# One block up to the output projection, score maxima of two groups inside the last projection steps, and pieces three slots later

## The reference, cut to what matters

```python
x = x + xattn(layernorm(x), ctx)        # x, ctx: [4, 1024, 512], fp32, 16 heads of 32
x = x + ffn(layernorm(x))
# xattn: q = x@Wq+bq, k = ctx@Wk+bk, v = ctx@Wv+bv
#   scores = q k^T / sqrt(32), -inf where masked, softmax over keys, @ v, @ Wo + bo
#   mask: three image chunks of 256 tokens attend within themselves; the last 256 (text)
#   tokens attend to all 768 image tokens and causally to text
# ffn: xq = fakequant(x)  with scale = sigmoid(clip) * max|x| / 127 over the WHOLE tensor
#   h = fakequant(silu(xq@Wg') * (xq@Wu'))  with a scale over the whole of h
#   out = h @ Wd'; Wg', Wu', Wd' are quantised row by row (1408 hidden units)
```

## Time and profile before

| | us |
|---|---|
| median of three runs (lowest, highest) | 1152.42 (1151.9, 1155.57) |
| the profiled execution | 1155.27 |
| its span, first to last instruction | 1153.5 |
| PE busy | 1062.2 (92%) |
| DVE / POOL / ACT busy | 750.1 / 640.9 / 512.5 |

### The profile page before, as it was taken

One profiled execution on the slowest core, in us unless ns is written; L12 is line 12 of the kernel. 1 busy time (PEld: TensorE's weight loads), 2 busy tenths in 40 slices (PEclk: granted clock), 3 DMA queues, 4 the chain that ended last, 5 costly groups with the idle time before them and its releaser, 6 DMA issues. The chain is left out here.

```text
span 1153.5 us, 18187 instructions
## 1 busy us (share of the span) xinstructions
PE 1062.2 (92%) x6527; PEld 704.8 (61%) x6550; DVE 750.1 (65%) x1340; ACT 512.5 (44%) x881; POOL 640.9 (56%) x345
## 2 busy tenths in 40 slices
PE   5999999999629989999999999899995799998898
PEld 4888888888516656666666666456763444443343
DVE  5665456654319757777777777236968477877785
ACT  3322223222101656666777666651110555553553
POOL 3434455344440979999999999555753113100373
PEclk9999999999955989999999999899997799999899
DMA  5987777856699896768888673449996353100876
GB/s 203 318 258 234 221 276 256 270 170 197 207 178 188 187 225 150 180 158 180 182 180 194 151 178 101 124 126 236 312 287 172 96 224 122 36 1 3 322 240 219
DMA packets 129619, 218.08 MB, mean 189 GB/s; under 512 B 29320, under 2 KB 55688, under 8 KB 128330
## 3 DMA queue, kind: packets, MB, share of 16 engines
q1 hardware_dynamic: 129546, 217.12, 68.1%
HBM read 134.76 MB, written 77.74 MB: 184 GB/s over the span
## 5 line engine op out<-in xcount | busy, mean ns | idle before, releaser
L775 ACT ACTIVATE a_probs<-a_banks 128x512 f32<-128x512 f32 (+2 forms) x512 | 233.9, 535 | 131.6 <-PE a_banks L991 106.6
L712 POOL TENSOR_TENSOR a_pair_sums<-a_probs,a_probs 128x2048 f32<-128x2048 f32 x48 | 223.6, 4658 | 66.3 <-ACT a_probs L775 57.6
L850 DVE TENSOR_REDUCE a_max<-a_banks 128x2 f32<-128x512 f32 x192 | 123.3, 685 | 53.8 <-PE a_banks L962 53.5
L991 PE MATMUL a_banks<-a_queries,a_keys 97*128 97x512 f32 x384 | 148.1, 429 | 10.4 <-ACT a_probs L775 5.7
L962 PE MATMUL a_banks<-a_keys,a_queries 96*128 96x256 f32 x384 | 86.0, 319 | 32.7 <-DMA a_queries<-q_split 32.7
L967 PE MATMUL a_banks<-a_keys,a_queries 96*128 96x512 f32 (+1 forms) x256 | 114.7, 462 | 0.0
L846 DVE CUSTOM_DVE_ANT_0 a_masked_scores<-a_banks,kept_mask 128x384 f32<-128x384 f32 (+1 forms) x128 | 79.5, 621 | 50.0 <-PE a_banks L967 49.7
L850 DVE TENSOR_REDUCE a_max_parts<-a_banks 128x1 f32<-128x512 f32 x128 | 87.9, 687 | 24.8 <-PE a_banks L967 20.9
L962 PEld LDWEIGHTS a_banks<-a_keys,a_queries 96*128 96x128 f32 x384 | 70.3, 205 | 54.5 <-DMA a_queries<-q_split 33.4
L1347 POOL TENSOR_TENSOR d_out<-d_out,f_x 128x512 f32<-128x512 f32 x28 | 42.6, 1548 | 99.1 <-DVE d_out L1375 99.1
L225 POOL TENSOR_SCALAR p_x<-p_x,p_neg_mean,p_rstd 128x512 f32<-128x512 f32 x32 | 28.2, 895 | 121.9 <-DVE p_rstd L330 121.9
(11 more groups left out here) (166 smaller groups left out, 2205.2 us busy)
## 6 DMA issues: line engine op xcount, KB each, us to landing
a_keys<-k_split SPq DMA_DIRECT2D x48, 512.0 KB, 8.5
a_queries<-q_split SPq DMA_DIRECT2D x48, 512.0 KB, 14.3
f_x<-x_scratch SPq DMA_DIRECT2D x14, 1024.0 KB, 7.8
p_c<-in_ctx_dram SPq DMA_DIRECT2D x8, 1024.0 KB, 8.8
p_x<-in_x_dram SPq DMA_DIRECT2D x8, 1024.0 KB, 10.9
v_scratch<-p_v_stage SPq DMA_DIRECT2D x16, 512.0 KB, 9.0
k_split<-p_stage_hi SPq DMA_DIRECT2D x16, 512.0 KB, 4.3
k_split<-p_stage_lo SPq DMA_DIRECT2D x16, 512.0 KB, 5.4
```

The costliest lines, as they stand in the source:

```text
L712: pool.tensor_tensor(PP[u % 2], PR[2 * c % 4], PR[(2 * c + 1) % 4], ALU.add).then_inc(paired, 1)
L775: act.activation(PR[kt % 4][:, j, 0:w], STB[:, n % NST, 0:w], ACT.Exp, scale=SCALE).then_inc(edone, 1)
L850: dve.tensor_reduce(out, src, AX.X, ALU.max).then_inc(wfree, 1)
L991: op = pe.matmul(out.rearrange("p (c t) -> p c t", t=SIT), keys, q, start=True, stop=True)
```

## The change

It does five things. (1) `project` and `attend_output` become one block, each engine running the first's instructions and then the second's without a meeting between. For that their memory is laid out anew: the projection has five banks instead of eight (the other three are the work banks of the pieces), one context buffer instead of two, one transposed pair each instead of two, two stage pairs for k and q together instead of four. (2) The 56 pieces of groups 0 and 1 and the turning of group 0's maxima go between the v and q items of steps 5, 6 and 7; their stacks are loaded part by part in steps 4 to 6. The keys of stack 1 lie where the x buffer and the context buffer are, and are loaded last in step 6. (3) The layernorm is cut in two (`moments`, `deviations`), which go behind the first and second k item. (4) Pieces start three slots later: those of group g run from slot 3 of group g-2 to slot 2 of group g-1; the turning is at slot 3; `shift_rows(i+1)` comes behind the store of slot 3. (5) In the feed-forward, the first chunk is quantised and turned in halves, one of the two copies behind it goes to DVE, the last group of h maxima is cut in two, and the first quantisation of `down` starts with one tile.

```diff
+NB = 5
+EARLY = 4
-TURN_SLOT = 1
+TURN_SLOT = 3
-GROUPS = ((0, 4), (4, 8), (8, IT))
+GROUPS = ((0, 4), (4, 8), (8, IT - 1), (IT - 1, IT))
+DOWN = [((0, 1), (1, 4), (4, 8), (8, IT))] + [((0, 4), (4, 8), (8, IT))] * (NCH - 1)
...
 # project, sync: step(b, u), late = n - 4 in steps 4 to 7
+                if late == 0:
+                    for q in sout:
+                        sp.wait_ge(q, 32 * 5)
                 for i in range(2):
                     s.reach(sp, free, NB + at(n) + VALUE + 2 * i + 2)
...
+                    if last and i == 0:
+                        A.shift_rows(sp, 0)
+                    A.load_early(sp, late, i)
...
+                stage_store(n, 0)
+                stage_store(n, 1)
+                A.load_early(sp, late, 2)
+                if last:
+                    for q in vout:
+                        sp.wait_ge(q, 16 * (NCH + 1))
+                    for i in range(2):
+                        A.load_values(sp, i)
+                    for part in range(3):
+                        A.load_stack(sp, 2, part)
+                if more(n, 2):
+                    s.reach(sp, free, NB + at(n) + CTURN + KT)
+                    load_c(n + 2)
+                stage_store(n, 2)
+                A.load_early(sp, late, 3)
+                stage_store(n, 3)
+                if late == 2:
+                    sp.wait_ge(full, at(n) + CTURN + KT)
+                    for part in range(3):
+                        A.load_stack(sp, 1, part)
+                if last:
+                    for part in range(3, 6):
+                        A.load_stack(sp, 2, part)
 # project, vector: step
                     dve.tensor_tensor(VST[t // 2][:, t % 2, :], bank(u, VALUE + t), BV, ALU.add).then_inc(free, 1)
+                    for i, k in A.early(n, t):
+                        A.largest(dve, i, k)
+                    if t == 0 and not more(n, 1):
+                        A.rows_out(dve, 0)
...
-                    layernorm(1 - u, n + 2, b if u == 0 else b + 1)
                 for j in range(KT):
-                    staged(u, n, KEY + j, j, 0, 1, KT + j)
+                    staged(u, n, KEY + j, j, 1, KT + j)
+                    if more(n, 1) and j == 0:
+                        moments(1 - u, n + 2, b + u)
+                    if more(n, 1) and j == 1:
+                        deviations(1 - u, n + 2)
                     ffn_rows(n, j)
 # project, tensor: step
                 for t in range(TT):
                     tokens_out("v", CT, t, claim(u, n, VALUE + t))
+                    for i, k in A.early(n, t):
+                        A.scores(pe, i, k)
+                    if t == 0 and not more(n, 1):
+                        A.turn_maxima(pe, 0)
...
 # attend_output
+        FIRST = [(n, item) for n, items in ((EARLY + 1, range(KT, 2 * KT)), (EARLY + 2, range(2 * KT)), (EARLY + 3, range(2 * KT)))
+                 for item in items]
+        COUNT = (3, 2, 2) * 4 + (4,) * 4 + (3,) * 4
-        def slot_pieces(kt):
-            first = sum(S_PER_SLOT[:kt])
-            return list(range(first, first + S_PER_SLOT[kt]))
+        def slot_pieces(i, kt):
+            slot = NKT * i + kt - TURN_SLOT
+            g, part = 2 + slot // NKT, slot % NKT
+            if slot < 0 or g >= NGRP:
+                return []
+            count = [S_PER_SLOT[(m + TURN_SLOT) % NKT] for m in range(NKT)]
+            first = sum(count[:part])
+            return [(g, k) for k in range(first, first + count[part])]
+        def load_early(sp, late, place):
+            part = 4 * late + place if late is not None else 9
+            if part < 6:
+                load_stack(sp, 0, part)
+            elif part < 9:
+                load_stack(sp, 1, part - 3)
 # attend_output, sync
-            for i in range(2):
-                load_stacks(i)
-                load_values(i)
-            shift_rows(0)
-            load_stacks(2)
-            load_values(2)
             for i in range(NGRP):
-                if i + 1 < NGRP:
-                    shift_rows(i + 1)
                 if i == 0:
-                    load_stacks(3)
-                    load_values(3)
+                    front.ffn_last(sp)
                 store(i, 0)
...
                 store(i, 1)
+                if i + 1 < NGRP:
+                    shift_rows(sp, i + 1)
+                if i == 0:
+                    for row in range(6):
+                        load_stack(sp, 3, row)
+                    sp.wait_ge(front.fst, 32 * (NCH + 1))
+                    for m in range(2, 4):
+                        load_values(sp, m)
...
                 sp.wait_ge(stfull, HG * NKT * (i + 1))
                 if i + 4 < NGRP:
-                    load_stacks(i + 4)
+                    for row in range(6):
+                        load_stack(sp, i + 4, row)
 # gate_up, tensor: the first chunk in halves
+            def turn_first():
+                for h in range(2):
+                    pe.wait_ge(xq, h + 1)
+                    for i in range(2):
+                        for k in range(2):
+                            for t in range(2 * h, 2 * h + 2):
+                                op = pe.transpose(TB[:, i, k, t * P:(t + 1) * P],
+                                                  XQ[0][:, t, (2 * i + k) * P:(2 * i + k + 1) * P], K.ident_b[:])
+                        if h:
+                            op.then_inc(turned, 1)
```

More of the change, by code:

```diff
@@ new lines, with __init__, place, stack @@
+S_ITEMS = 7
+S_PER_SLOT = (3, 3, 4, 4, 4, 3, 4, 3)
+TURN_SLOT = 3
+AHEAD = 3
+QROWS = 3 * DH
+NGRP = BATCH * G
+NST, NWK = 3, 3
+STACK, TILE = HG * N, KT * C
+GROUPS = ((0, 4), (4, 8), (8, IT - 1), (IT - 1, IT))
+DOWN = [((0, 1), (1, 4), (4, 8), (8, IT))] + [((0, 4), (4, 8), (8, IT))] * (NCH - 1)
+RES = 6
+class Kept:
+    pass
+class Memory:
+    def __init__(self, s):
+        self.nc, self.at = s.nc, {}
+        for name, words in (("arena_a", RES * IT * CH), ("arena_b", 9 * TILE)):
+            s.sb(name, [P, words])
+            self.at[name] = s.nc.sbuf_base - 4 * words
+    def place(self, name, arena, word, shape, dt=F32):
+        return self.nc.alloc_sbuf_tensor_at(name, shape, dt, offset=self.at[arena] + 4 * word)[:]
+    def stack(self, name, i, half, word, shape, dt=F32):
+        return self.place(name, "arena_a", (2 * i + half) * STACK + word, shape, dt)
+    def rest(self, name, word, shape, dt=F32):
+        return self.place(name, "arena_a", 8 * STACK + word, shape, dt)
+    def over(self, name, word, shape, dt=F32):
+        return self.place(name, "arena_b", word, shape, dt)
@@ L181, in step @@
                     load_x(n + 2, u)
-                for i in range(4):
-                    item = KEY + 2 * i if i < 2 else query(final) + 2 * (i - 2)
-                    s.reach(sp, free, NB + at(n) + item + 2)
-                    dst = (ks, ks, qs, qs)[i]
-                    for part in range(2):
-                        d = dst[part].rearrange("(m p) t -> p m t", p=P)[:, 2 * (i % 2):2 * (i % 2) + 2, bass.ds(n * CH, CH)]
-                        sp.dma_start(d, f32(STG[i][part][:])).then_inc(sout[i], 16)
@@ new lines, in attend_output, with early @@
+        FIRST = [(n, item) for n, items in ((EARLY + 1, range(KT, 2 * KT)), (EARLY + 2, range(2 * KT)), (EARLY + 3, range(2 * KT)))
+                 for item in items]
+        COUNT = (3, 2, 2) * 4 + (4,) * 4 + (3,) * 4
+        def early(n, item):
+            if not isinstance(n, int) or (n, item) not in FIRST:
+                return ()
+            at = FIRST.index((n, item))
+            first = sum(COUNT[:at])
+            return [divmod(k, NPC) for k in range(first, first + COUNT[at])]
@@ L698, in _, with gpsimd @@
             sp.wait_ge(ldk, 32)
[L700 to L703 removed]
+        A.sync = sync
+        def gpsimd(pool, front):
             def pair(i, c):
@@ new lines, in attend_output, with scores @@
+        A.vector = vector
+        def scores(pe, i, k):
+            n = A.pieces
+            j, m = PIECES[k]
+            if k == 0:
+                pe.wait_ge(stk[i % 4], LOADS * (i // 4 + 1))
+            pe.wait_ge(wfree, n + 1)
+            out = WB[:, n % NWK, :]
+            keys = KS[i % 4][0:QROWS, j, :]
+            queries = lambda t: QS[i % 4][0:QROWS, j, t * P:(t + 1) * P]
+            if m < 3:
+                for half in range(2):
+                    op = pe.matmul(out[:, half * SIT:(half + 1) * SIT], queries(2 * m + half),
+                                   keys[:, m * SIT:(m + 1) * SIT], start=True, stop=True)
+            else:
+                t, part = 6 + (m - 3) // 2, (m - 3) % 2
+                k0, k1 = 512 * part, min(512 * (part + 1), (t + 1) * P)
+                op = pe.matmul(out[:, 0:k1 - k0], queries(t), keys[:, k0:k1], start=True, stop=True)
+            op.then_inc(wfull, 1)
+            A.pieces += 1
@@ L1004, in values @@
                     pe.wait_ge(ifree, 3 * i + kt // 2)
+                if kt == 0 and i == 0:
+                    for bank in (6, 7):
```

(3 more changed lines are left out.)

618 lines of the change are left out of this document (315 added, 303 removed).

## The result

The changed kernel takes 1199.88 us (median of 4 runs, 1196.25 to 1203.79) against 1153.54 for the kernel before: a ratio of 1.039, 95% interval 1.037 to 1.042. The forecast was 1156.5, with a range of 8 in 10 that ended at 1167. The number is wrong by 43 us; the sign is right, at a chance of 48% that the forecast gave it. The profiled run has 1196.25, its span 1194.5.

What follows compares the result with a forecast made beforehand. PE, busy 92% of the span, was taken to bound the kernel. The terms -22.9 + 8.8 + 19.8 + 2 - 3.6 = +4.1 moved the median from 1152.4 to 1156.5 us; range of 8 in 10: 1138 to 1167.

Steps and rivals of the forecast that it cites:

- Five banks: Projection steps 0 to 6: with five banks PE starts q 1.8 us late in each step, 12.6 us in all.
- Pieces between items: Between projection items: pieces with changes to and fro cost 14 us, waits for DVE and the turning 3.4 us.
- Keys of stack 1: Projection step 7: PE waits 10 us for these keys, plus 1.5 us of low clock, together 11.5 us.
- Last piece to group 1's second pass: Between these two points: burst of scores, slots and one wait take 20 us, against 24.7 before.
- the third rival: Queue shared with the projection gets worse: stores land late, ACT waits for stage buffers, +10 us, 1166.5; chance 13%.
- The backlog: Shift rows of group 2 come some 11 us late behind queued loads; groups 1 to 3 lose 8.8 us.
- What every group pays: Groups 3 to 14: waits of 0.9 us at the turning and 0.9 for shift rows, 19.8 us lost.
- Feed-forward: Quantisation in halves wins 1.7 us before the first matmul, a one-tile start in down 1.9; together -3.6 us.
- the first fell: Rival: waits in the groups, at slots 3 and 5, don't show; at most 0.3 us a group, 1140; chance 15%.
- the second fell: Rival: five banks are enough in the projection, DVE's order costs nothing, 1144 us; chance 14%.

Runs made afterwards that it cites:

- the best version: The kernel of e10, the fastest of all the runs: 1120.44 us, ratio 0.969 to the kernel before.
- e9: Changed kernel with shift rows before the store, pieces two slots later, stack 1 keys earlier, stacks one group later, layernorm before k items: 1126.97 us, ratio 0.975.
- e10: e9 with the key parts of stack 2 issued right behind the last step's v stores, ahead of the k stores: 1120.44 us, ratio 0.969.
- e5: Changed kernel with the key parts of stack 2 issued behind the last two q stores instead of ahead: 1196.41 us, ratio 1.037.
- e4: Changed kernel with stacks loaded one group later, behind the shift rows instead of ahead of them: 1180.93 us, ratio 1.023.
- e1: Changed kernel with the shift rows issued ahead of the output store that they followed: 1168.41 us, ratio 1.012.
- e2: Changed kernel with pieces two slots later instead of three, the turning staying at slot 3: 1182.23 us, ratio 1.027.
- e6: Changed kernel with moments, deviations and ACT's root ahead of the k items again, still with five banks: 1186.31 us, ratio 1.027.
- e7: Kernel before with only the pieces three slots later, the turning at slot 3 and shift rows behind slot 3's store: 1195.52 us, ratio 1.034.
- e13: e10 with shift rows behind slot 3's store again and one 512 KB stack part between them in groups 1 to 12: 1202.15 us, ratio 1.042.
- e3: Changed kernel with the keys of stack 1 issued ahead of both q stores of step 6: 1183.05 us, ratio 1.026.

## Why the prediction was wrong

**Five banks** (12.6 us). The wait was there in steps 0 to 6, for the reason given: 1.3 + 0.4 a step. Measured 2.1 a step (38.26 against 36.17), 14.7 for seven, and 3.3 more in the two steps whose clock fell: 5.4 too little. The layernorm ahead again takes 1.5 to 1.7 of the 2.1 away.

**Pieces between items** (17.4). Nearly right. In the best version the stretch from the x transposes of step 5 to the first score takes 121.9 us; before, to 307.2, it took 95.9. Of the 26.0 between them 3.2 are bank waits in step 5, some 1.2 are longer steps, and 3.3 are the clock, which was low in step 5 behind those waits (clock 0.93 in the row above; the transposes behind the waits took 1.2 us more than elsewhere, the q items behind them 1.9 and 0.2). That leaves 18.3: 3.7 of waits for DVE (3.4 forecast) and 14.6 for columns and changes (14). By the same working the changed kernel has 19.6 (131.7 - 95.9, less 12.0 for the keys and 4.2 for the banks).

**Keys of stack 1** (11.5). Right: 10.7 of wait and 1.3 of clock behind it, 12.0, for 10 and 1.5.

**Last piece to group 1's second pass** (20). This step failed by mechanism: 29.2 us. I had charged the burst, the slots and one wait, and given the moved transfers room on the queue "in the last step". The room was there, but just behind it 2.5 MB stood ahead of the last q store, and the new memory had put POOL's pair sums over the buffer that this store reads. That was the third rival's mechanism, at 13%, with ACT and POOL's place swapped. The kernels with other orders of stack 2 show it (e9: 28.2 us with a wait of 8.1 for POOL; e10: 24.4 with 4.1), and e5 shows that moving the load only behind the store moves the wait. The other part of the miss is a clock that I had charged at nothing: even the 24.4 us of the best version have a granted clock of 0.86.

**The backlog** (11 of wait). Right in kind, 14.9 measured; with the clock behind it 6.1 us too little for the two stretches. e4 shows the cause.

**What every group pays** (1.8). The two waits were 0.76 and 0.64 for 0.9 and 0.9, and a regular group 26.2 for 26.1. That this comes out so close is partly luck: the waits are 0.4 shorter, and each costs 0.2 to 0.3 beside its length, which I hadn't charged. What failed is that I took all eleven as regular. The landing of the shift rows isn't a constant: in five of the eleven stretches it was late, or the clock fell behind it, and these took 27.4 to 28.1 us, 8.0 more than five times 26.1. The forecast's own high bound of 1.7 for each wait would have given it. Before the change a whole slot or two of slack stood ahead of each of these two steps, and PE had no wait at either in groups 4 to 14; the change had used the slack up. Group 14 (34.8 for 31.6) is the same, with a wait of 1.77 and a clock of 0.81.

**Feed-forward** (-3.6). Right: from the first quantisation to the end it is 253.3 us for 257.4, 4.1 won, and `down`'s wait for ACT is 1.8 instead of 3.90. The stretch ahead of it, from group 15's first score through the output projection, took 154.7 us for 152.4, for which the forecast had nothing (PE's waits for DVE there are 6.0 for 4.3); no run tests why.

**The rivals.** The waits in the groups do show (e1, e2), so the first fell; five banks weren't enough in this order (8.8 and 3.0 us of waits, which e6 takes away but for 2.8), so the second fell too. The range ended at 1167, which was the third rival's time alone; with the high bounds of the other terms on top (2.5 a step for the banks, 1.7 for each wait in a group, 15 for the backlog) it would have reached some 1195 (4.9 + 17.6 + 6.2 more).

Open is why shift rows land late in some groups. In the changed kernel it was groups 3, 6, 10 and 14: the transfer is issued as far ahead of PE's want as elsewhere and takes 3.1 to 3.8 us to land instead of 2.2. Groups 6, 10 and 14 are those with a small store of reciprocals (`reciprocals<-a_recs`) a few us ahead, and in e4, e5 and e6 they are the same three; but that store has landed before the shift rows are issued (528.86 + 1.5 against 532.60), and in e2 and e7 groups without it are late. So this is no more than a lead. Open too is what decides, for waits between 1.3 and 2.3 us, whether the clock falls.

## What to carry to other kernels

Where an engine is full, a step moved right behind the one that it depends on turns slack into a wait in every turn of the loop, and a small late transfer into several us; leave it the slack of its slowest case, not of its median. When a stage is overlapped with the next, list what the new memory layout makes wait for stores that are still in the queue, and where each large load stands ahead of a small urgent transfer. A change of several parts should be undone part by part: here it was 46 us slower as a whole, and with five places mended and one load moved it is 36 us faster than the kernel before.

## What the runs showed of the hardware

The granted clock fell in all twelve groups with a wait of 3.6 us or more (e13). For shorter ones it fell or it didn't: over all profiles and their groups 1 to 13, the longest wait of a group was between 1.2 and 2.4 us 25 times, and behind 18 of these the clock fell (the shortest 1.26 in e7 and 1.29 in e5), behind 7 it stayed at 1.00 (the longest 2.15 in e2 and 2.32 in e3). Behind waits up to 1.12 it never fell. The Trainium skill ("TensorE: Matmul & The Clock Gate", "HAM oscillation — how this bites in real kernels") describes a loop in which a wait for data in each turn brings the low clock back each time; e13 agrees, at some 2.5 us a group (its twelve groups take 77.7 us more than those of the best version, for 48.1 of waits). I had not expected that projection steps with waits of 1.3 and 0.5 us fall in some executions (the changed kernel's, e2, e5: 0.96, 1.6 us each) and not in others (e1, e4).
